# An eight-layer transformer-like kernel on one core: attention weights folded once, routing results stored once, and steps of the sparse-attention stage in another order

## The reference

```python
    def _L1_xattn_ref(q, k, Wq, Wk, Wv, Wo):      # q = layernorm(x), k = context
        query = q @ Wq.T
        key_p = k @ Wk.T
        value = k @ Wv.T
        sim = jnp.einsum('bqd,bkd->bqk', query, key_p)
        mean = jnp.mean(sim, axis=(1, 2), keepdims=True)
        var = jnp.var(sim, axis=(1, 2), keepdims=True)
        sim = (sim - mean) * jax.lax.rsqrt(var + EPS)
        attn = jax.nn.softmax(sim, axis=-1)
        out = jnp.einsum('bqk,bkd->bqd', attn, value)
        return out @ Wo.T
```

```python
        logits = jax.nn.relu(x @ rw1 + rb1) @ rw2 + rb2
        vals, ids = jax.lax.top_k(logits, K)                 # K = 2
        probs = jax.nn.softmax(vals, axis=-1)
        m = jax.nn.one_hot(ids_f, E, dtype=jnp.int32)        # ids_f: ids of all rows in a line
        pos = jnp.cumsum(m, axis=0) - 1
        keep = (pos_tok < CAP).astype(x.dtype)
```

## Time and profile before

| | |
|---|---|
| median of 3 runs | 5588.3 us (5583.16 to 5591.88) |
| the profiled execution | 5593.68 us, of which the profile's span is 5590.7 us |
| mean granted TensorE clock | 0.952 of full speed |
| PE busy | 4988.9 us, 89% of the span |
| DVE, ACT, POOL busy | 3221.9 us (58%), 1888.5 (34%), 1767.2 (32%) |
| a1 from its first statistics to its last result | 1334.90 to 1602.7 us |
| route | 1607 to 2062.44 us |
| fa | 3147 to about 4565 us |

### The profile page before, as it was taken

The page is one execution under the profiler, slowest core; times in us unless marked ns, Lnnn a source line. Parts: engine busy times, 40 slices in busy tenths (PEclk is TensorE's granted clock), DMA queues, the critical chain, the costliest instruction groups (busy, mean ns, idle before and its releaser), DMA issues. The chain is left out here.

```text
span 5590.7 us, 100571 instructions
## 1 busy us (share of the span) xinstructions
PE 4988.9 (89%) x32588; PEld 3916.0 (70%) x32588; DVE 3221.9 (58%) x9783; ACT 1888.5 (34%) x3986; POOL 1767.2 (32%) x2213
## 2 busy tenths in 40 slices
PE   7888859997988969996999699999999977999978
PEld 4555548886976758885666488878878854777845
DVE  5666658775533333313888377777777763544444
ACT  2333313333432322322555243333333323222224
POOL 2111114442213343313544022222222220566522
PEclk9999979998998889998999799999999989999989
DMA  1100011112321122222222110011000008222223
GB/s 40 32 28 28 22 38 46 49 49 70 113 84 34 42 68 67 66 65 67 69 72 65 66 33 28 29 29 33 27 27 29 29 14 276 85 90 90 77 88 107
DMA packets 321098, 331.84 MB, mean 59 GB/s; under 512 B 65797, under 2 KB 289002, under 8 KB 317706
## 3 DMA queue, kind: packets, MB, share of 16 engines
q1 hardware_dynamic: 307466, 302.60, 17.4%
q0 software_dynamic: 13312, 25.25, 1.9%
HBM read 234.72 MB, written 93.03 MB: 59 GB/s over the span
## 5 line engine op out<-in xcount | busy, mean ns | idle before, releaser
L2512 PE MATMUL fa_h<-fa_xnT,fa_w 128*128 128x256 f32 x2048 | 491.1, 386 | 0.0
L2524 PE MATMUL fa_y<-fa_w,fa_hT 128*128 128x256 f32 x2048 | 462.5, 379 | 0.0
L2524 PEld LDWEIGHTS fa_y<-fa_w,fa_hT 128*128 128x128 f32 x2048 | 386.8, 190 | 76.6 <-issue 26.1
L2512 PEld LDWEIGHTS fa_h<-fa_xnT,fa_w 128*128 128x128 f32 x2048 | 390.0, 193 | 52.8 <-ACT fa_hT L2391 0.3
L2391 ACT ACTIVATE fa_hT<-fa_h,fa_b 128x256 f32<-128x256 f32 x512 | 215.0, 471 | 519.3 <-PE fa_h L2512 423.6
L420 DVE TENSOR_REDUCE a_mx<-a_score 128x16 f32<-128x1920 f32 x128 | 276.1, 2157 | 158.9 <-PE a_score L594 158.9
L1001 PE MATMUL f_c_ps<-f_hs,f_diag 128*128 128x256 f32 x1536 | 355.1, 384 | 11.8 <-DVE f_hs L869 9.0
L1001 PEld LDWEIGHTS f_c_ps<-f_hs,f_diag 128*128 128x128 f32 x1536 | 284.3, 190 | 62.0 <-issue 15.9
L527 ACT ACTIVATE a_pT<-a_score 120x2048 f32<-120x2048 f32 x128 | 240.4, 1878 | 184.3 <-PE a_score L651 125.9
L1535 PE MATMUL r_h<-r_xnT,r_rw 128*128 128x256 f32 x1024 | 283.0, 432 | 0.7 <-ACT r_xnT L1485 0.7
L135 POOL TENSOR_SCALAR a_rs<-a_mv 128x2 f32<-128x2 f32 x96 | 21.2, 221 | 724.1 <-DVE a_mv L129 724.0
(11 more groups left out here) (459 smaller groups left out, 11211.5 us busy)
## 6 DMA issues: line engine op xcount, KB each, us to landing
cv_toep<-kernels SPq DMA_DIRECT2D x16, 2048.0 KB, 9.4
x<-a_xo SPq DMA_DIRECT2D x96, 256.0 KB, 3.2
f_xb<-x SPq DMA_DIRECT2D x64, 256.0 KB, 2.8
f_xres<-x SPq DMA_DIRECT2D x64, 256.0 KB, 2.8
a_xb<-x SPq DMA_DIRECT2D x64, 256.0 KB, 3.5
e_w<-in_L_ffn_ew SPq DMA_DIRECT2D x16, 1024.0 KB, 7.0
a_cb<-in_ctx SPq DMA_DIRECT2D x96, 90.0 KB, 3.0
a_xb<-in_x SPq DMA_DIRECT2D x32, 256.0 KB, 3.1
```

Of the source, the lines that this page charges most:

```text
L2512: last = pe.matmul(h_ps[j % 2][:, c, :], w1[:, e, k, f:f + P], xnT[it.p][:, k, :], start=k == 0, stop=k == KD - 1)
L2524: last = pe.matmul(bank[:, t * D:(t + 1) * D], hT[e % 2][:, k, t * P:(t + 1) * P], w2[:, e, k, :], start=k == 0, stop=k == KE - 1)
```

## The change

Four things are done.

1. In a1, PE multiplies the weights with each other at the start of the stage (`qk` from Wk and Wq, `vo` from Wv and Wo, 16 matmuls), so that scores are formed from the normed x and `g` = qk x context, and the result from the probabilities and `u` = vo x context. `project_q`, `project_o` and the copies to `qT` and `oT` are gone. Scores and results have two PSUM banks each, `u` four buffers. `score_spread` is split: the shift is its own step. All orders change, and four slots are written into a loop instead of two.
2. In route, `read_at` and `wgt` hold all samples, `store_meta` is gone, and two stores of 64 KB stand at the end. The count takes two matmul steps instead of five.
3. In fa, `turn_sum`, `project` and `scores` stand later on PE, some ACT steps with them; the large weights are loaded behind x(1), not x(0).
4. The host lays out layer 1's weights untransposed.

```diff
@@ normed_attention
+    qk, vo = st.sb("qk", [CP, 2, D]), st.sb("vo", [CP, 2, D])
...
+    u = [st.sb(f"u{p}", [SK, D]) for p in range(4)]
...
+    s_ps, y_ps = ([st.ps(f"{n}{p}", [P, 512]) for p in two] for n in ("s", "y"))
...
-    MOM, SPR = 4, 5
+    MOM, SPR = 4, 3
...
+    sched = dict(unroll=4, history=4)
...
-            pipeline(sp, B, DEPTH, [(9, store), (2, load_context), (6, load_residual), (0, load)])
+            pipeline(sp, B, DEPTH, [(9, store), (2, load_context), (7, load_residual), (0, load)], **sched)
...
-            pipeline(pool, B, DEPTH, [(5, score_root), (1, roots_of)])
+            pipeline(pool, B, DEPTH, [(6, score_root), (1, roots_of)], **sched)
...
+            def score_shift(it):
+                p = it.p
                 dve.wait_ge(root_ready, 2 * it.i + 2)
...
-                c.add(dve.tensor_scalar(shift[p][:], mx[p][:], root[p][:], -1.0, ALU.mult, ALU.mult))
-                c.add(dve.tensor_copy(var[p][:], root[p][:]))
+                dve.tensor_scalar(shift[p][:], mx[p][:], root[p][:], -1.0, ALU.mult, ALU.mult).then_inc(shifted, 1)
...
-            pipeline(dve, B, DEPTH, [(8, y_out), (6, reciprocal), (5, score_moments), (2, norm), (5, score_spread), (1, norm_stats)])
+            pipeline(dve, B, DEPTH, [(6, score_spread), (1, norm_stats), (5, score_moments), (6, score_shift), (8, y_out), (2, norm),
+                                     (7, reciprocal)], **sched)
...
+            for n, (out, bank) in enumerate(((qk, s_ps), (vo, y_ps))):
+                act.wait_ge(folded, n + 1)
+                for half in two:
+                    act.copy(out[:, half, :], bank[half][0:CP, 0:D]).then_inc(fold_out, 1)
...
             pe.wait_ge(weights, 64)
+
+            for left, right, bank in ((wk, wq, s_ps), (wv, wo, y_ps)):
+                for half in two:
+                    for k in range(KD):
+                        last = pe.matmul(bank[half][0:CP, 0:D], left[:, k, half * CP:(half + 1) * CP], right[:, k, :], start=k == 0, stop=k == KD - 1)
+                last.then_inc(folded, 1)
+            pe.wait_ge(fold_out, 4)
...
-            def project_q(it):
...
-                last.then_inc(q_done, 1)
-
...
-                        last = pe.matmul(s_ps[:, t * SK:(t + 1) * SK], qT[it.p][:, k, t * P:(t + 1) * P], kT[it.p][:, k, :],
+                        last = pe.matmul(s_ps[it.p][:, t * SK:(t + 1) * SK], xnT[it.p][:, k, t * P:(t + 1) * P], g[it.p][:, k, :],
...
-            def project_o(it):
...
+                for t in range(TL):
+                    last = pe.matmul(y_ps[it.p][:, t * D:(t + 1) * D], prT[it.p][:, t, :], u[it.at][:], start=True, stop=True)
                 last.then_inc(y_done, 1)
...
-            pipeline(pe, B, DEPTH, [
-                (8, project_o), (3, turn_x), (7, attend), (5, scores), (4, project_kv), (5, sum_moments), (6, turn_p),
-                (4, project_q)])
+            pipeline(pe, B, DEPTH, [(5, scores), (8, attend), (3, turn_x), (7, turn_p), (4, project_context), (5, sum_moments)], **sched)
@@ route
+    read_at, wgt = st.sb("read_at", [P, B, TL, 2], U32), st.sb("wgt", [P, B, TL, 2])
...
-            def store_meta(it):
-                sp.wait_ge(placed, PLC * (it.i + 1))
-                sp.dma_start(meta_at[it.i], read_at[it.p][:].rearrange("p t r -> p (t r)")).then_inc(meta_out[it.p], 16)
-                sp.dma_start(meta_w[it.i], wgt[it.p][:].rearrange("p t r -> p (t r)")).then_inc(meta_out[it.p], 16)
-
-            pipeline(sp, B, DEPTH, [(0, load), (3, store_xn), (8, store_meta)])
+            pipeline(sp, B, DEPTH, [(0, load), (3, store_xn)])
+            sp.wait_ge(placed, PLC * B)
+            sp.dma_start(meta_at.rearrange("b p r -> p b r"), read_at[:].rearrange("p b t r -> p b (t r)")).then_inc(meta_out, 16)
+            sp.dma_start(meta_w.rearrange("b p r -> p b r"), wgt[:].rearrange("p b t r -> p b (t r)")).then_inc(meta_out, 16)
...
-                    dve.wait_ge(meta_out[p], 32 * it.h)
                     dve.wait_ge(scattered[p], 64 * it.h)
...
-            pipeline(dve, B, DEPTH, [(7, place_choices), (5, choose), (1, norm_stats), (6, select), (2, norm)])
+            pipeline(dve, B, DEPTH, [(6, select), (2, norm), (7, place_choices), (5, choose), (1, norm_stats)])
...
-                pe.wait_ge(chosen, CHO * it.i + 3)
+                pe.wait_ge(chosen, CHO * it.i + 4)
...
-                pe.matmul(n_ps[:, 0:NE], const["ones"][:], count[p][:], start=True, stop=False)
-                pe.matmul(n_ps[:, 0:NE], const["tri"][:], sel[p][:, 0, :], start=False, stop=True)
-                pe.matmul(n_ps[:, NE:2 * NE], const["ones"][:], count[p][:], start=True, stop=False)
-                pe.matmul(n_ps[:, NE:2 * NE], const["ones"][:], sel[p][:, 0, :], start=False, stop=False)
-                pe.matmul(n_ps[:, NE:2 * NE], const["tri"][:], sel[p][:, 1, :], start=False, stop=True).then_inc(n_done, 1)
+                flat = lambda a: a[it.p][:].rearrange("p t e -> p (t e)")
+                pe.matmul(n_ps[:, 0:TL * NE], const["ones"][:], flat(count), start=True, stop=False)
+                pe.matmul(n_ps[:, 0:TL * NE], const["tri"][:], flat(sel), start=False, stop=True).then_inc(n_done, 1)
@@ adaptive_with_sparse_attention
-                if opening(it):
+                if isinstance(it.i, int) and it.i == 1:
                     for a, n in ((w1, "ew1"), (w2, "ew2")):
                         sp.dma_start(a[:], w[n]).then_inc(large, 16)
...
-                (4, d_out), (5, relu(0)), (5, relu(1)), (5, relu(2)), (6, xT3_out), (6, scale_rows), (5, relu(3)), (6, k_out), (6, q_out),
-                (4, exps), (5, relu(4)), (5, relu(5)), (7, aT_out), (5, relu(6)), (7, cT_copy), (5, relu(7)), (6, head_exps(0)),
+                (4, d_out), (5, relu(0)), (5, relu(1)), (5, relu(2)), (5, relu(3)), (6, xT3_out), (6, scale_rows), (4, exps), (5, relu(4)),
+                (6, k_out), (6, q_out), (5, relu(5)), (7, aT_out), (5, relu(6)), (7, cT_copy), (5, relu(7)), (6, head_exps(0)),
...
-                (4, difficulty), (5, up(0)), (4, gates), (5, up(1)), (5, up(2)), (5, bias), (6, turn_sum), (5, up(3)), (6, project),
-                (5, up(4)), (5, down(0)), (6, scores), (5, down(1)), (5, up(5)), (4, turn_weights), (7, mean_heads), (5, up(6)), (7, attend),
+                (4, difficulty), (5, up(0)), (4, gates), (5, up(1)), (5, up(2)), (5, bias), (5, up(3)), (6, turn_sum),
+                (5, up(4)), (5, down(0)), (6, project), (5, down(1)), (6, scores), (5, up(5)), (4, turn_weights), (7, mean_heads), (5, up(6)), (7, attend),
```

More of the change, by code:

```diff
@@ L1042, in normed_attention @@
     rs = [st.sb(f"rs{p}", [P, TL]) for p in two]
[L1043 to L1045 removed]
+    xnT = [st.sb(f"xnT{p}", [P, KD, S]) for p in two]
+    g = [st.sb(f"g{p}", [P, KD, SK]) for p in two]
+    u = [st.sb(f"u{p}", [SK, D]) for p in range(4)]
     sst = [st.sb(f"sst{p}", [P, 6]) for p in two]
@@ L1304, in route @@
     at = [st.sb(f"at{p}", [P, TL, NE], U32) for p in two]
-    atf, prob, keep, place, wgt = ([st.sb(f"{n}{p}", [P, TL, 2]) for p in two] for n in ("atf", "prob", "keep", "place", "wgt"))
+    atf, prob, keep, place = ([st.sb(f"{n}{p}", [P, TL, 2]) for p in two] for n in ("atf", "prob", "keep", "place"))
     gap, ex = ([st.sb(f"{n}{p}", [P, TL]) for p in two] for n in ("gap", "ex"))
@@ L1308, in route @@
     spot = [st.sb(f"spot{p}", [P, TL, 2, NE]) for p in two]
-    sel, count = ([st.sb(f"{n}{p}", s) for p in two] for n, s in (("sel", [P, TL, NE]), ("count", [P, NE])))
+    sel, count = ([st.sb(f"{n}{p}", [P, TL, NE]) for p in two] for n in ("sel", "count"))
     slot = [st.sb(f"slot{p}", [P, TL, 2], U32) for p in two]
-    read_at = [st.sb(f"read_at{p}", [P, TL, 2], U32) for p in two]
+    read_at, wgt = st.sb("read_at", [P, B, TL, 2], U32), st.sb("wgt", [P, B, TL, 2])
     tok = [st.sb(f"tok{p}", [P, TL], I32) for p in two]
@@ L1317, in route @@
     weights, filled, emptied = (st.sem(n) for n in ("weights", "filled", "emptied"))
-    x_in, xn_out, meta_out = ([st.sem(f"{n}{p}") for p in two] for n in ("x_in", "xn_out", "meta_out"))
+    x_in, xn_out = ([st.sem(f"{n}{p}") for p in two] for n in ("x_in", "xn_out"))
+    meta_out = st.sem("meta_out")
     scattered = const["rows_placed"]
@@ L1462, in place_choices @@
                 if it.reused():
-                    dve.wait_ge(meta_out[p], 32 * it.h)
                     dve.wait_ge(scattered[p], 64 * it.h)
-                c.add(dve.tensor_copy(read_at[p][:], place[p][:]))
+                rows = (lambda a: a[:, it.i] if isinstance(it.i, int) else a[:, bass.ds(it.i, 1)].rearrange("p o t r -> p (o t) r"))
+                c.add(dve.tensor_copy(rows(read_at), place[p][:]))
                 c.add(dve.scalar_tensor_tensor(place[p][:], keep[p][:], float(2 * NE * CAP), place[p][:], ALU.mult, ALU.add))
```

113 lines of the change are left out of this document (50 added, 63 removed).

## The result

The changed kernel takes 5453.1 us (median of 4 runs, 5445.8 to 5455.7) against 5590.1 us (median of 4, one run more than stands behind the 5588.3 given ahead): a ratio of 0.9751, 95% interval 0.9733 to 0.9769, or 137 us less. The forecast was 5463 us, said as 5462. The profiled execution has a span of 5453.9 us against 5590.7, so the two traces can be compared stage by stage. A stage is taken here from its first load (for experts its first gather, for m, the stage behind cv, its first matmul into `m_h`) to that of the next.

What follows compares the result with a forecast made beforehand. PE, busy 89%, bounds the kernel: a1 PE-bound, fa PE-bound with small holes, route held by waits. −16 (a1) − 96 (route) − 13 (fa) = −125 from 5588.3 us gives 5463 us, said as 5462; range 5415 to 5520.

Steps and rivals of the forecast that it cites:

- 7.3 us: a1: new slot from 4.15 us norm_stats to norm plus a 3.15 us load round trip, against 7.83; −16 us.
- the 8.1 us slot: a1: slot if all of PE's slot work ran at half clock after idling; +8 us instead of −16.
- DVE waits at the first store into read_at 24 times for 169.0 us: Route: small stores hold DVE 7.0 us each time; ending this wait cuts the slot from 13.18 us, −109 with shorter count.
- is there a slot's front early: Route: with select first on DVE, the count's operand is ready early; no separate size given.
- slot of 9.65 us: Route: PE's 10.31 us slot less 0.68 for three fewer count pairs, against 13.18; −109 us over 31 slots.
- Rival 3: Route: another wait replaces the small stores', the cast waiting for scatters; half the gain goes, −48, 5510 us; chance 0.10.
- The end stores: End of route: two 64 KB stores take about 19 us, the last scatter hides 6 to 8; +13 us.
- Rival 5: Route: slower, end stores cost what the small ones' waits cost, 225 us for 32 pairs in series; 5675 us; chance 0.03.
- takes away most of the clock loss: 6 × 1.5 = −9: fa: turn_sum behind up(3) leaves 0.6 us of wait and ends most slow-clock up runs; −9 us.
- What the text said of the waits: fa: what turn_sum no longer waits, mean_heads will, as DVE's chain stays late; cadence stays over 42 us.
- Rival 4: fa gives the full stall back; 5436 us; chance 0.08.
- The fill: Start of fa: x(1), 14.38 us late behind the large weights, is now issued ahead of them; about −4 us.

Runs made afterwards that it cites:

- e13: Kernel before with route's small stores gathered into two at the end and their wait gone, all orders and the count as before: 5581.3 us, 0.9991 of before.
- e12: Kernel before with only route's DVE order changed, plus one wait that order needs; small stores and five-pair count stay: 5492.3 us, 0.9826 of before.
- e1: Kernel before with the a1 part of the change alone (normed_attention and host layout): 5541.2 us, 0.9913 of before.
- e4: Changed kernel with fa as before the change, so the a1 and route parts only: 5440.1 us, 0.9728 of before.
- e9: Kernel before with 116 one-column memsets of an unread tile put on DVE at the start of fa: 5568.6 us, 0.9968 of before.
- e3: Kernel before with the fa part of the change alone: 5586.4 us, 0.9996 of before.

## Why the prediction was right, and where it was not

**The total** (−126 forecast, −137 measured, inside the range) is nearer than its parts deserve. Route and fa rest on a wrong cause, and most of what a1 gave comes from a term that was left out. That they add up so well is luck.

**a1, −16 forecast, −19.3 measured.** The mechanism was right: DVE waits for one load of x in each slot, 2.9 us against the 2.2 to 2.6 said. But it gave a third of its sum: the loads' own span fell by 5.5 us (225.6 to 220.1). The step that took the slot as "7.3 us" from "with 3.15" had the landing right (3.13 us in the mean of the last 22 slots) and the way from stats to norm nearly so (4.10 against 4.15). It left out the 0.38 us that lie in the mean between norm and the issue of x, most of them in the five slots in which load_context, ahead of x, had waited for PE; the slot is 7.65. The larger part, 13.3 us, is the drain, the end of the stage in which nothing is loaded any more, and no term stood for it: from the last load of x to the last y_out it was 1602.2 − 1555.8 = 46.4 us, with PE busy 43.6 of them, and is 1581.3 − 1548.2 = 33.1, with PE busy 25.3. The lower clock was mostly lost in the slack as expected: it is 0.84, not 0.5, and PE is busy 76% of the time, where 55 to 65% was looked for. Whether at full clock PE's context step would have come sooner in those five slots (6 us in all) no run shows. The Trainium skill's rule ("TensorE: Matmul & The Clock Gate", HAM oscillation) on tiles that wait agrees as far as the clock falls; the 8.1 us slot that the prediction made of it did not come.

**Route, −96 forecast, −84.8 measured.** The step that failed is "DVE waits at the first store into read_at 24 times for 169.0 us", read as the price of those stores. Without them 17.7 us went (e13), 31.7 in the slots themselves. The order of DVE, which the prediction priced only as an operand that "is there a slot's front early", gave 63.7 (e12). The forecast came near because its slot of 9.65 us was PE's own work, and the change does reach it (9.4), by the order. Rival 3, another wait at the same place, was right in kind and not in the place: norm, not the cast, waits for its store, 42.4 us in all, which made five slots 24 us longer, more than all by which the forecast was too hopeful. It was given 0.10.

**The end stores, +13 forecast, +7.1 measured.** The pieces of the earlier trace rows were the right guide: 10.7 and 17.1 us to landing, where about 19 for both was said, and the last scatter hid 10 us of it (1935.08 to 1945.08) and not 6 to 8. The Trainium skill's fit ("DMA: Bandwidth & Descriptors", Anatomy of one DMA — SWDGE (gpsimd) path) would give an estimate of 2.2 us for 64 KB; the page has it for DMAs that GpSimd issues, and these are issued by SP in pieces of 16 B, so the measured times decide. In other kernels with these stores the end costs 7.1 to 8.5 us, in e13 12.4. Rival 5 had no ground.

**fa, −13 forecast, −24.8 measured.** The working took the two pauses of the earlier trace rows as given and counted what turn_sum would save. One pause went by itself, with the code of the stages ahead (e1, e4, e9), and took 24 to 31 us with it. The step that failed is "takes away most of the clock loss: 6 × 1.5 = −9": with both pauses there the edit left the slot at 42.74 us (42.75 before), and its −4.9 lies at the two ends of the stage. With one pause it costs 0.40 us a slot, +6.2 in the stage. What the text said of the waits held: mean_heads became the one that waits, 20.2 us in e3 where turn_sum had waited 21.2, and 22 times 0.5 us in the changed kernel. The slot there is 42.09 us, by the pause that went. Rival 4 came near in time and not in reason. The fill was nearly right: from the first load of x to the first up it was 37.8 us and is 33.0, for −4 said, and of these 4.8 us 2.7 are left at the first copy of the earlier trace rows.

## What to carry to other kernels

A wait that is long and frequent isn't the price of what is waited for: take it away alone before believing it, since in a loop across engines the slack lands on whichever wait comes last. When engines run lists of steps in order, look for a step that needs another engine's result of the same slot (choose, select, count; load of x behind load_context), and move it a slot apart; more buffers did little until that was done. And compare unedited stages: fa changed by 2% while its code stood still, because the place of the code was in the measurement. Where a loop has a pause with releaser "issue" in every round, ask the DMA view of just that stretch for instruction packets.

## What the runs showed that was not expected

The same DVE instructions of fa have two pauses, one, one and a short one, or one of double length in every second slot, by where they lie in the program, and each pause over 2 us has a packet of the instruction queue in it. In e13, where fa is longest, there is one pause but of 5.1 us (waits of DVE, 3300 to 4200; then the instruction queue in one of them, 3450.48 to 3455.44):

```profile
DVE fa_st L125 <- issue: 45.9, 9, 5.4
```

```profile
q14 instruction: 2, 0.02, 0.8%
```

The place of the code moves fa, with its code as before, between 1424.9 and 1473.4 us, up to 48 us or 0.9% of the kernel, more than most edits here; 116 idle memsets were worth 20 us. Scatters of 4 B pieces raise the landing of 256 KB stores beside them from 3.0 to 5.2 us in the median and from 3.3 to 14.7 at the most. Two stores of 4096 pieces of 16 B take 10.7 and 17.1 us.
